# Ranks of routed tokens: running sums on VectorE and three matmuls per group

## What is computed

```python
gate = softmax(flat_x @ w_gate.T)                 # 4096 tokens, 8 experts
topk_scores, topk_idx = top_k(gate, 2)
cw = (one_hot(topk_idx, 8) * topk_scores[..., None]).sum(axis=1)
h = gelu(einsum('td,edh->teh', flat_x, W1) + b1)
y = einsum('teh,ehd->ted', h, W2) + b2
out = einsum('ted,te->td', y, cw)
```

## Time and profile before

| | |
|---|---|
| median of 3 runs | 2216.92 us (2213.29 to 2218.58) |
| profiled execution, first to last instruction (span) | 2218.2 us |
| PE busy | 1862.6 us (84%) |
| DVE busy | 1573.0 us (71%) |
| ACT busy | 1392.0 us (63%) |
| POOL busy | 1284.7 us (58%) |
| mean granted TensorE clock | 0.924 |

### The profile page before, as it was taken

How to read it: one execution, slowest core, us unless ns; L and a number is a source line. 1 busy time by engine, 2 the same in 40 slices (tenths; PEclk the granted TensorE clock), 3 DMA queues, 4 the chain that set the end, 5 groups by cost and what they waited for, 6 DMA issues and landing times. The chain is left out here.

```text
span 2218.2 us, 51508 instructions
## 1 busy us (share of the span) xinstructions
PE 1862.6 (84%) x16704; PEld 1411.6 (64%) x16705; DVE 1573.0 (71%) x2848; ACT 1392.0 (63%) x3948; POOL 1284.7 (58%) x1099
## 2 busy tenths in 40 slices
PE   4169957716996699999999999675899999999996
PEld 4158842515884377777777776342677777777774
DVE  4548858644886588878778887243788878788883
ACT  5125543212554478887888877365688788878874
POOL 4354410246442587878878786101887878778771
PEclk9979979657997699999999999787999999999999
DMA  6212140021214211101011010000111111110111
GB/s 202 68 58 61 44 108 15 18 75 59 66 44 113 74 25 28 24 21 28 21 28 25 21 27 18 4 0 3 33 24 23 24 23 28 25 25 21 26 23 38
DMA packets 87308, 88.26 MB, mean 40 GB/s; under 512 B 13978, under 2 KB 65863, under 8 KB 87016
## 3 DMA queue, kind: packets, MB, share of 16 engines
q1 hardware_dynamic: 77288, 68.09, 12.1%
q0 software_dynamic: 8704, 17.85, 2.4%
q10 hardware_dynamic: 1152, 0.25, 0.1%
HBM read 35.60 MB, written 22.22 MB: 26 GB/s over the span
## 5 line engine op out<-in xcount | busy, mean ns | idle before, releaser
L2037 POOL TENSOR_TENSOR mac_probs<-mac_probs,mac_prec 128x512 f32<-128x512 f32 x256 | 265.5, 1043 | 204.4 <-DVE mac_prec L1852 203.6
L1713 ACT ACTIVATE mac_probs<-banks,mac_nmax 128x128 f32<-128x128 f32 x1024 | 359.6, 386 | 0.2
L1809 DVE TENSOR_TENSOR route_pool<-banks,tables 128x1024 f32<-128x1024 f32 x256 | 301.0, 1217 | 36.2 <-ACT route_pool L1673 31.7
L2017 POOL TENSOR_TENSOR route_pool<-route_pool 128x1024 f32<-128x1024 f32 x128 | 303.2, 2369 | 39.0 <-DVE route_pool L1809 15.8
L1843 DVE TENSOR_REDUCE mac_nmax<-banks 128x4 f32<-128x512 f32 x256 | 164.9, 686 | 139.0 <-PE banks L1541 139.0
L2028 POOL TENSOR_TENSOR mac_qkn<-route_pool,mac_rc 128x1024 f32<-128x1024 f32 x128 | 243.9, 1905 | 16.6 <-issue 7.6
L854 POOL DMA_INDIRECT x_sorted<-route_pool,route_index x128 | 124.5, 973 | 217.1 <-DVE route_index L666 122.7
L862 POOL DMA_INDIRECT y_tokens<-moe_bench,moe_goal x144 | 140.9, 979 | 178.9 <-DVE moe_bench L805 132.2
L1713 ACT ACTIVATION_READ_ACCUMULATOR mac_probs<-banks,mac_nmax 128x1 f32 x1024 | 231.8, 226 | 0.0
L54 PE MATMUL banks<-wqkv_h,mac_hh 128*128 128x512 f32 x384 | 179.8, 468 | 26.4 <-POOL mac_hl L1992 21.4
L388 PE MATMUL banks<-w,moe_gh 128*128 x576 | 163.3, 360 | 44.9 <-issue 26.9
(11 more groups left out here) (315 smaller groups left out, 5069.1 us busy)
## 6 DMA issues: line engine op xcount, KB each, us to landing
mac_v_even<-mac_v SPq DMA_DIRECT2D x224, 128.0 KB, 2.2
moe_xs<-x_sorted SPq DMA_DIRECT2D x144, 72.0 KB
route_pool<-y_tokens SPq DMA_DIRECT2D x16, 512.0 KB, 7.2
y_tokens<-moe_bench,moe_goal POOLq DMA_INDIRECT x144, 2.3
moe_bench<-in_L_attn_x SPq DMA_DIRECT2D x8, 256.0 KB, 5.4
route_pool<-in_L_ffn_W SPq DMA_DIRECT2D x4, 512.0 KB, 7.0
x_sorted<-route_pool,route_index POOLq DMA_INDIRECT x128
b<-in_b_flat SPq DMA_DIRECT2D x1, 2048.0 KB
```

Of the source, the lines that this page charges most:

```text
L1713: e = act.activation(probs[:, r, p, :], m.ps[:, S + r, p * P:(p + 1) * P], ACT.Exp, bias=nmax[:, r, p:p + 1], accum_out=psum[:, r, p:p + 1])
L1809: turn = dve.tensor_tensor(turned[:, i, :, :].rearrange("q k (h s j) -> q k h s j", s=2, j=DH // 2), q[:, :, :, ::-1, :] if i else q, tabl ...
L2017: pool.tensor_tensor(sums[:], turned[:, 0, :, :], turned[:, 1, :, :], ALU.add).then_inc(added, 1)
L2037: pool.tensor_tensor(probs[:, r, :, :], probs[:, r, :, :], prec[:, r, :].unsqueeze(2).to_broadcast([P, HP, P]), ALU.mult).then_inc(shared[ ...
```

## The change

`select` still makes `chosen`, now behind a pad of 8 zero tiles. Behind it VectorE makes running sums over the tiles by doubling: it adds to each tile the one 1 before it, then 2, 4 and 8 before it (strides 1 and 2 for four tiles, 1 to 8 for twelve and sixteen), in turns between the two halves of a new bf16 buffer `before`, which has the same pad of zeros. Each add waits for the one before; the last raises `selected`. The sums are at most 16 and exact in bf16. `ranks` then needs three matmuls per group: the triangle on `chosen`, the ones on the running sums moved by one tile (all tiles before), and the ones on the last tile's running sum (the group's totals). Two memsets per app write the pads.

```diff
--- before.py
+++ after.py
@@ -232,6 +232,8 @@
     HALF = GROUPS.index((NH_SEQ, NB))
     AT = [sum((hi - lo) * TT * NE + NE for lo, hi in GROUPS[:i]) for i in range(len(GROUPS))]
     MOST = max(hi - lo for lo, hi in GROUPS) * TT
+    PAD = MOST // 2
+    strides = lambda n: [1 << j for j in range((n - 1).bit_length())]
     group_of = [i for i, (lo, hi) in enumerate(GROUPS) for b in range(lo, hi)]
     first = app == 0
     with Phase(nc) as c:
@@ -260,7 +262,8 @@
         gap, weight = sb("gap", [P, NB * TT, NE]), sb("weight", [P, NB * TT, NE])
         peak, second, marked_at = sb("peak", [P, MOST]), sb("second", [P, MOST]), sb("marked_at", [P, MOST])
         vote, rest = sb("vote", [P, MOST, NE]), sb("rest", [P, MOST, NE])
-        picked, chosen = sb("picked", [P, TOP, NB * TT, NE]), sb("chosen", [P, MOST, NE], BF16)
+        picked = sb("picked", [P, TOP, NB * TT, NE])
+        chosen, before = sb("chosen", [P, PAD + MOST, NE], BF16), sb("before", [P, 2, PAD + MOST, NE], BF16)
         got, place = sb("got", [P, TOP, MOST, NE]), sb("place", [P, TOP, MOST])
         given = bench[:, :TOP * NB * TT * NE].rearrange("q (k s e) -> q k s e", k=TOP, e=NE)
         gsum = sb("gsum", [P, TOP, NB * TT])
@@ -338,17 +341,15 @@
             def ranks(i):
 
                 n = (GROUPS[i][1] - GROUPS[i][0]) * TT
-                flat = lambda lo, hi: chosen[:, lo:hi, :].rearrange("q t e -> q (t e)")
+                bank, to = PB[i % len(PB)], AT[i] + n * NE
+                flat = lambda t, lo: t[:, lo:lo + n, :].rearrange("q t e -> q (t e)")
+                sums = before[:, (len(strides(n)) - 1) % 2, :, :]
                 pe.wait_ge(selected, START + i + 1)
                 if i >= len(PB):
                     pe.wait_ge(indexed, START + i - len(PB) + 1)
-                pe.matmul(m.ps[:, PB[i % len(PB)], AT[i]:AT[i] + n * NE], m.low_bf[:], flat(0, n), start=True, stop=False)
-                for t in range(1, n):
-                    pe.matmul(m.ps[:, PB[i % len(PB)], AT[i] + t * NE:AT[i] + n * NE], m.ones_bf[:], flat(0, n - t), start=False, stop=t == n - 1)
-                for t in range(n):
-                    mm = pe.matmul(m.ps[:, PB[i % len(PB)], AT[i] + n * NE:AT[i] + (n + 1) * NE], m.ones_bf[:], chosen[:, t, :], start=t == 0,
-                                   stop=t == n - 1)
-                mm.then_inc(ranked, 1)
+                pe.matmul(m.ps[:, bank, AT[i]:to], m.low_bf[:], flat(chosen, PAD), start=True, stop=False)
+                pe.matmul(m.ps[:, bank, AT[i]:to], m.ones_bf[:], flat(sums, PAD - 1), start=False, stop=True)
+                pe.matmul(m.ps[:, bank, to:to + NE], m.ones_bf[:], sums[:, PAD + n - 1, :], start=True, stop=True).then_inc(ranked, 1)
 
             def turn_x(i, k):
 
@@ -627,7 +628,14 @@
                 step(dve.tensor_tensor(won[:, 1], v, wide(at), ALU.is_equal))
                 if i:
                     dve.wait_ge(ranked, START + i)
-                dve.tensor_tensor(chosen[:, :n, :], won[:, 0], won[:, 1], ALU.add).then_inc(selected, 1)
+                step(dve.tensor_tensor(chosen[:, PAD:PAD + n, :], won[:, 0], won[:, 1], ALU.add))
+                part = chosen
+                for j, s in enumerate(strides(n)):
+                    part, last = before[:, j % 2, :, :], part
+                    sm = dve.tensor_tensor(part[:, PAD:PAD + n, :], last[:, PAD:PAD + n, :], last[:, PAD - s:PAD - s + n, :], ALU.add)
+                    if s != strides(n)[-1]:
+                        step(sm)
+                sm.then_inc(selected, 1)
 
             def shares():
 
@@ -731,6 +739,8 @@
                 dve.memset(m.eps[:], LN_EPS)
                 dve.memset(m.ones_bf[:], 1.0)
                 dve.memset(m.mean_of[:], 1.0 / P).then_inc(blanked, 1)
+            step(dve.memset(chosen[:, :PAD, :], 0.0), False)
+            step(dve.memset(before[:, :, :PAD, :], 0.0), False)
             step(dve.memset(route.owner[:, :GROUP], 0), False)
             step(dve.memset(route.rows[:, :GROUP], 0), False)
             means(0)
```

## The result

The changed kernel takes 2218.96 us (median of 20 runs, 2213.15 to 2228.25), the kernel before 2215.36 (20 runs, 2209.52 to 2218.58): ratio 1.002 [1.0011, 1.003]. No gain, at the edge of what can be measured as a loss. The forecast of 2182 us was wrong; that 2218.96 still touches the stated range, whose upper end is 2219, is due to case D alone. The profiled execution has a span of 2214.2 us, 4 us under that of before; that execution took 2215.93 us, 3 us under the median, so its places are used and not its sum.

What follows compares the result with a forecast made beforehand. The prediction took VectorE's wait for PE's late `ranked` signal to be on the path. App 0 -17.9 and app 1 -17.3 made -35.2 us, span 2218.2 to 2183.0, less 1.3 to the median: 2182 us, range 2176 to 2219.

Steps and rivals of the forecast that it cites:

- case D: Rival: signal comes at a set distance behind GpSimd's batch, adds vanish in the hole; 2217.5 us, chance 0.21.
- The hole and its wait: Before the last `positions(HALF)`, VectorE idles 17.12 and 15.57 us for `ranked`, stuck by a matmul burst during sends.
- The adds: VectorE's running sums: at most 0.45, 1.16 and 1.30 us in first, middle and last group.
- case C: Rival: sends hold VectorE's adds, 0.97 us each, 15.5 us on the path; 2197 us, a small chance, 0.05.
- Matmuls: The last group's three matmuls in `ranks` make about 0.4 us.
- Middle group: L659 follows the adds at once if the signal is prompt: -4.1 us in app 0, -3.4 in app 1.
- What is late next: Behind the middle group, PE and ScalarE: last L459 at 32.3 instead of 34.86; last group gains 2.5 us, app 1 3.4.
- Last group: Idle time falls to 0.4 us, adds cost 1.30: -15.4 and -13.9 us; with the earlier gains -17.9 and -17.3.
- What stands behind the tables: SP's first load in app 1, there at 470.1 us, before the last norm at 470.7: hidden, 0.6 us to spare.
- app 1's first load becomes the end of the chain: Sign stated beforehand: if that load ends the chain in app 1, the prediction is wrong.
- near 471 us: Sign: where PE's first L358, its first expert matmul, should start in app 1; near 75 us in app 0.
- E: Rival: the wait has a fixed length from `selected` on, adds stand before it; 4.9 us slower, 2222 us, chance 0.09.

Runs made afterwards that it cites:

- b_scored: The kernel before, with GpSimd's first sends held until PE has scored all sequences: 2217.71 us, 1.001 of the kernel before.
- a_scored: The changed kernel, with GpSimd's first sends held until PE has scored all sequences: 2214.13 us, 0.9993 of the kernel before.
- a_pause: The changed kernel, with GpSimd waiting after each sequence of the first half until its eight sends have landed: 2192.22 us, 0.99 of the kernel before.
- b_held: The kernel before, with all GpSimd sends held until the last group's index is made: 2233.61 us, 1.0086 of the kernel before.
- a_third: The changed kernel, unchanged, on the chip where the kernel before takes 2142.98 us: 2146.66 us, 1.0018 of it.
- b_again: The kernel before, unchanged, measured and traced once more: 1.0002 of the kernel before, which took 2216.65 us.
- b_pause: The kernel before, with GpSimd's landing wait after each first-half sequence, on the chip where it takes 2142.92 us without: 2153.86 us, 1.0057.
- old_mid: The changed kernel with the old matmuls back in the first and middle groups, running sums in the last only: 2208.92 us, 0.9964 of the kernel before.

## Why the prediction was wrong

**The hole and its wait**: right. It was `ranked`, and it cost what the profile showed; the burst of 32 is signalled late amid sends and three matmuls are not (b_scored, a_scored).

**The adds**: the price was an upper bound, as said. 0.17 us each for 32 columns, 0.21 for 96 and 0.23 for 128, spaced 0.21, 0.24 and 0.26, so 0.42, 0.93 and 1.0 us instead of 0.45, 1.16 and 1.30. In the middle group they ran amid sends (25.05 to 25.98 us) at that pace, so case C fell. The rule of the Trainium skill, SBUF — State Buffer, "Who interferes with whom", by which a VectorE instruction with two SBUF inputs contends with a GpSimd instruction that reads SBUF, doesn't show in these rows. It does show where C did not look for it, with the send as the one that waits: 8.13 us for one send beside VectorE's L733 and L735 in a_pause, 10.13 us in b_held, 0.97 for most others, while VectorE's steps took the 1.2 us that they take in the changed kernel with no send beside them.

**Matmuls**: 0.50 us from the last add to L667, predicted 0.4.

**Middle group**: predicted -4.1 and -3.4 us. L667 starts at 26.95 instead of 30.61 (-3.7), in app 1 18.2 us after the app's start instead of 21.5 (-3.3). Right.

**What is late next**: this step failed. "Late next in app 0 are PE and ScalarE ... so the last L459 comes at 32.3 instead of 34.86." It was worked out from durations, as if PE's signals behind the new `ranks` were prompt; the last copy came at 46.98. In a_third, where signals are prompt, it comes at 32.07, so the sum was right for a chip like that. The evidence had been there: the L459 at 31.35 with 9.60 us idle was put down to the burst ahead of it, and the prompt L459 at 34.86 was read as "sends alone don't do it". But GpSimd had stopped between 30.01 and 32.26, just when those signals were due. The rows held the gap, and the sum never asked what closes it.

**Last group**: predicted -17.9 us in app 0 and -17.3 in app 1 in all. The idle time at `positions(HALF)` went as forecast, and came back at `gates(HALF)` and L596: counted from the app's start, L667 moved by -5.4 and +4.9 us.

**What stands behind the tables**: "hidden, with 0.6 us to spare" was right that the loads are close. In a_pause and a_third, where the tables are early enough, the first tile does wait for them (57.7 us from app 1's start in a_third; the forecast was 488.01 - 17.3 - 412.8 = 57.9). By the prediction's own sign (app 1's first load becomes the end of the chain) it would have been wrong in this step even where signals are prompt. The first L358 "near 471 us" leaves out what app 0 was to gain; with it, the forecast was 453. For app 0 the prediction didn't work out the loads, and in a_third the first tile waits for the loads too: 72.0 us from the start where 88.2 - 17.9 = 70.3 was forecast, with the send of 10.13 us ahead of it. The expert stretches show no sign of growing for an earlier start (226.5 against 228.2 us in app 0, and 223.7 in b_again).

**The rivals**: D's time, 2217.5 us, is the nearest to the 2218.96 that came, and its core, that the sends have a part in the hole, was right. That is partly luck. Its test failed: the wait that it named was prompt, no wait ended 3.8 us behind the 32nd send, and the adds did not vanish in the hole. Against the kernel before, measured beside it, the change is +3.6 us, between D's +0.6 and E's +4.9; but E's fixed wait at `positions(HALF)` is gone from the changed kernel and from b_held. The same section of the Trainium skill says that TensorE and ScalarE never wait on anyone. It speaks of the ports of SBUF, and the runs leave it untouched for the work itself (the transposes take 1.09 us in the changed kernel as in the earlier trace rows). Taken as a rule on signals, as the prediction took it, it would have spoken against the late signals altogether; yet they are what the rows show, and they decided the time.

**Where signals are prompt** the change costs 0.18% (a_third). The 32 sends are on the path to SP's first load there, in app 0 with one send of 10.13 us, and in app 1 the first send starts 11.1 us after the app's memset instead of 10.7 (b_pause), behind the first group's adds. That is 0.4 us of the 3.7; the rest is open, the more so as the kernel before has no trace from that chip.

**Open**: whether the closed gap by itself took the gain. For it speak old_mid, where a gap of 1.56 us comes back and `gates(HALF)` starts 7.9 us sooner in app 0 than in the changed kernel, and the landing waits; the gap alone was never measured where signals are late. Open too: what makes one signal late and another prompt on the same chip. In the changed kernel the transposes that ended at 27.33 were signalled within 0.1 us amid sends, those that ended at 32.24 took 14.7. And why one of the chips doesn't show it.

## What to carry to other kernels

When a wait is put down to something that disturbs signals, ask of every other signal in the same stretch what lets it through now, and whether the change keeps that. A delay that looks like pure loss may be what makes room: here a late index gave GpSimd a gap of 1.5 to 2.3 us, and speeding it up closed the gap. Ask also what a faster engine will now run beside: here the sends met VectorE's L733 and L735 and one of them took 8 to 11 us. Where GpSimd issues long runs of indirect DMAs beside short PE work, try a landing wait every eight sends (0.99 on two chips), and measure it on more than one chip: where signals are prompt it costs 0.6% (b_pause).

## What the runs showed of the hardware that was not expected

- On chips where the kernel before takes about 2216 us, completion signals of PE can come late, by up to 26 us, while GpSimd issues indirect sends one every 1.27 us, whether they stand behind 32 matmuls, 24 or four transposes. ScalarE and VectorE wait for them, and PE behind ScalarE's late copies. Others amid the same sends are prompt.
- VectorE's own steps can be late too: in old_mid, with the sends running, the chain of `tables`, in which each step waits for the one before on the same engine, has 5.80 us of idle time at L714 (60.84 us), and 4.58 us in app 1. So it isn't only PE's signals.
- On another chip the same kernels show none of it and take 3.3% less; 16 to 22 us of the difference lie in each stretch of expert tiles (a_third against the changed kernel in the table).
- In both kinds GpSimd's sends mostly take 0.97 us, with 0.30 between them. The exception on both is a send beside VectorE's eight steps L733 and L735, which ends only when they do: 8.13 us in a_pause, 10.13 in b_held and a_third, with VectorE's steps as fast as without it.
